# A two-layer graph network: where the node update's own half, its gate and its last elementwise steps are computed

## What is computed

```python
h = jnp.maximum(_layernorm(x, axis=-1), 0.0)
em = jnp.concatenate([h[src], h[dst]], axis=-1)
em = jax.nn.relu(layer_norm(em @ msg_w + msg_b, msg_g, msg_beta)) * edge_weights[:, None]
messages = segment_sum(em, dst) / (counts + 1e-08) * (counts > 0)
gate = jax.nn.sigmoid(h @ gate_w + gate_b)
combined = jnp.concatenate([h, messages], axis=-1)
h_new = jax.nn.relu(layer_norm(combined @ upd_w + upd_b, upd_g, upd_beta))
x = x + gate * h_new + (1.0 - gate) * h
```

## Time and profile before

| | us |
|---|---|
| median of 3 runs | 2472.26 (2470.81 to 2472.52) |
| the profiled execution, its own time | 2471.0 |
| its span in the trace | 2469.2 |
| attention layer's and message loop's gathers, busy on POOL | 1624.4 |
| busy: PE, DVE, ACT, POOL | 1646.5, 1522.7, 982.5, 1683.3 |
| mean granted TensorE clock | 0.85 of full |

### The profile page before, as it was taken

The page is one execution under the profiler, slowest core; times in us unless marked ns, Lnnn a source line. Parts: engine busy times, 40 slices in busy tenths (PEclk is TensorE's granted clock), DMA queues, the critical chain, the costliest instruction groups (busy, mean ns, idle before and its releaser), DMA issues.

```text
span 2469.2 us, 44266 instructions
## 1 busy us (share of the span) xinstructions
PE 1646.5 (67%) x9934; PEld 1201.4 (49%) x9934; DVE 1522.7 (62%) x4806; ACT 982.5 (40%) x3715; POOL 1683.3 (68%) x1718
## 2 busy tenths in 40 slices
PE   2387778777877777777456666666666666666650
PEld 2255555555555555555344454454454455544550
DVE  5455555555555555555647766666676666667668
ACT  3244334333434343434444444444444344434420
POOL 3377777777777777776017777777777777777732
PEclk9799889898988998999677888888788888889885
DMA  8544344444444344343244444433444444344321
GB/s 257 138 91 86 91 91 87 91 90 90 88 89 91 85 92 89 87 91 72 58 121 98 86 89 92 92 87 89 92 91 86 91 92 92 83 92 93 76 56 52
DMA packets 207823, 228.62 MB, mean 93 GB/s; under 512 B 103103, under 2 KB 153684, under 8 KB 207701
## 3 DMA queue, kind: packets, MB, share of 16 engines
q0 software_dynamic: 54784, 115.94, 24.0%
q1 hardware_dynamic: 152598, 110.34, 16.4%
q10 hardware_dynamic: 384, 1.70, 0.3%
HBM read 194.60 MB, written 33.24 MB: 92 GB/s over the span
## 4 chain that ended last, share of the span: by engine, by line
POOL 56%; issue 19%; PE 8%; DMA 7%; DVE 5%; SPq 1%; ACT 1%; POOLq 1%; ACTq 0%; DVEq 0%
POOL room L667 56%; DMA room<-src_table,rec 5%; PE psum L774 2%; PE psum L704 1%; PE psum L756 1%; PE psum L746 1%; DMA node_x<-in_x 1%; DVE room L1557 1%; PE psum L741 1%; DMA room<-state 1%; DVE stats L1127 1%; PE psum L835 1%; SPq L457 1%; PE psum L764 0%; ACT room L1000 0%
## 5 line engine op out<-in xcount | busy, mean ns | idle before, releaser
L667 POOL DMA_INDIRECT room<-src_table,rec x1664 | 1624.4, 976 | 684.1 <-issue 495.3
L835 PE MATMUL psum<-room,ident 128*128 128x384 f32 (+1 forms) x512 | 292.6, 659 | 377.4 <-DMA room<-src_table,rec 297.9
L1050 ACT ACTIVATE room<-psum 128x128 f32<-128x128 f32 x832 | 218.8, 274 | 585.6 <-DVE room L1478 583.2
L1316 DVE TENSOR_TENSOR room<-psum,room 128x384 f32<-128x384 f32 (+1 forms) x256 | 151.1, 590 | 455.6 <-ACT room L982 367.8
L982 ACT ACTIVATE room<-psum 128x384 f32<-128x384 f32 (+1 forms) x256 | 132.1, 516 | 560.5 <-PE psum L746 557.4
L1478 DVE TENSOR_TENSOR room<-psum,msg_g 128x384 f32<-128x384 f32 (+1 forms) x256 | 151.0, 590 | 315.0 <-PE psum L840 312.8
L746 PE MATMUL psum<-ident,room 128*128 128x128 f32 x832 | 155.4, 305 | 207.4 <-DMA room<-src_table,rec 206.9
L835 PEld LDWEIGHTS psum<-room,ident 128*128 128x128 f32 x512 | 93.1, 227 | 409.7 <-issue 384.7
L853 PE MATMUL psum<-room 128*125 128x128 f32 x1664 | 285.2, 318 | 1.5 <-ACT room L1062 1.5
L774 PE MATMUL psum<-room 128*125 128x128 f32 x1664 | 262.2, 300 | 18.9 <-ACT room L1000 6.3
L840 PEld LDWEIGHTS psum<-room 125*128 125x128 bf16 x2496 | 195.4, 112 | 140.8 <-issue 123.8
(11 more groups left out here) (179 smaller groups left out, 2122.6 us busy)
## 6 DMA issues: line engine op xcount, KB each, us to landing
room<-dst_perm SPq DMA_DIRECT2D x128, 406.2 KB
room<-src_table,rec POOLq DMA_INDIRECT x1664
room<-dst_table SPq DMA_DIRECT2D x128, 62.5 KB
src_table<-room SPq DMA_DIRECT2D x24, 224.0 KB
dst_table<-room SPq DMA_DIRECT2D x24, 224.0 KB
st_in<-state SPq DMA_DIRECT2D x64, 64.0 KB
state<-st_out SPq DMA_DIRECT2D x64, 64.0 KB
st_in<-state SPq DMA_DIRECT2D x64, 62.5 KB
```

What stands on the lines that cost most here:

```text
L667: pool.indirect_dma_start(out=xg[:, u, t * P:(t + 1) * P], out_offset=None, in_=src_table[n][:, :], in_offset=bass.IndirectOffsetOnAxis(ap ...
L835: nc.tensor.matmul(msg_bank[b][:, cols], ident[:, :], xg[:, u, t0 * P:t1 * P], start=True, stop=False, skip_group_check=True)
L1050: i = nc.scalar.activation(sq[:, j * P:(j + 1) * P], msg_bank[b][:, j * P:(j + 1) * P], ACT.Square, accum_out=var_e[:, c, j:j + 1])
```

## The change

The own half and the gate move in front of the message loop, behind the second tables. PE's `update_own` makes `h @ [upd_w own half | gate_w]`, 129 columns, into `rows_ps`; ACT's `gate_of` makes the gate from the last column; DVE's `own_part` makes `rest = 1 - gate`, overwrites `node_h` with `relu(node_h) * rest`, adds that to `node_x`, and then overwrites `node_h` with own half plus `upd_b`. PE's first message waits for all of it (`s_zh`), and ACT and DVE have it in front of their first pair. At the end `update` has only the message half, and `add_own` adds `node_h` in place of `upd_b`. The norm goes from DVE to ACT (`norm_out`), the product with the gate from POOL to ACT (`relu_out`: relu with the gate as scale, as the gate is positive) for groups 0 to 9, and to DVE for groups 10 to 12 (gate times the rows plus `node_x`, then the maximum with `node_x`). POOL has nothing left at the end. ACT makes the norm of groups 0 to 4 between its copies of groups 7 to 11, and the rest after the last square root. `upd_w` is loaded in two DMAs in place of one, and one memset of a column is gone.

The diff, cut to its core:

```diff
@@ sync @@
-            (upd_w[:, :, 0:D], a["L1_gnn_upd_w"].rearrange("(h k) f -> k h f", h=2)),
-            (upd_w[:, 0, D:D + 1], a["L1_gnn_gate_w"]),
+            (upd_w[:, 0:D], a["L1_gnn_upd_w"][0:D, :]), (upd_m[:, :], a["L1_gnn_upd_w"][D:2 * D, :]),
+            (upd_w[:, D:D + 1], a["L1_gnn_gate_w"]),
@@ gpsimd @@
-            pool.wait_ge(s_hrelu, 1)
-            for g, (t0, t1) in enumerate(GROUPS):
-                pool.tensor_tensor(node_x[:, t0:t1, :], node_x[:, t0:t1, :], node_h[:, t0:t1, :], ALU.add).then_inc(s_xh, 1)
-            for g, (t0, t1) in enumerate(GROUPS):
-                n = t1 - t0
-                pool.wait_ge(s_ur, g + 1)
-                ge(pool, s_fin, g - 1)
-                pool.tensor_tensor(ug[0:PP, g % 2, 0:n, :], ur[0:PP, g % 2, 0:n, :],
-                                   gate[:, t0:t1].unsqueeze(2).to_broadcast([PP, n, D]), ALU.mult).then_inc(s_uh, 1)
@@ tensor @@
-            pe.wait_ge(s_row, 2 * NG)
+            def update_own(g):
+                t0, t1 = GROUPS[g]
+                pe.wait_ge(s_row, 2 * NG)
+                ge(pe, s_zh, g - 1)
+                for t in range(t0, t1):
+                    i = nc.tensor.matmul(rows_ps[g % 2][0:PP, t - t0, 0:D + 1], feat_h[:, t, :], upd_w[:, :], start=True, stop=True)
+                i.then_inc(s_u, 1)
+            pe.wait_ge(s_wb, NWB * 16)
+            for g in range(NG):
+                update_own(g)
+            pe.wait_ge(s_zh, NG)
             all_pairs(pe, msg_slot, last, 1)
...
                 ge(pe, s_z, g - 1)
-                ge(pe, s_gate, g - 1)
                 for t in range(t0, t1):
-                    to = rows_ps[g % 2][0:PP, t - t0, 0:D + 1]
-                    nc.tensor.matmul(to, feat_h[:, t, :], upd_w[:, 0, :], start=True, stop=False)
-                    i = nc.tensor.matmul(to, mt[:, g % 2, t - t0, 0:PP], upd_w[:, 1, :], start=False, stop=True)
+                    i = nc.tensor.matmul(rows_ps[g % 2][0:PP, t - t0, 0:D], mt[:, g % 2, t - t0, 0:PP], upd_m[:, :],
+                                         start=True, stop=True)
@@ scalar @@
+            for g in range(NG):
+                gate_of(g)
             split_high(msg, 0, 0)
...
+            def norm_out(g):
+                t0, t1 = GROUPS[g]
+                act.wait_ge(s_norm_scale, 4 + (1 if t1 <= HALVES[0][1] else 2))
+                for t in range(t0, t1):
+                    i = nc.scalar.activation(msum[0:PP, t, :], msum[0:PP, t, :], ACT.Identity, bias=nmr[:, t:t + 1],
+                                             scale=rstd[:, t:t + 1])
+                i.then_inc(s_un, 1)
+            def relu_out(g):
+                t0, t1 = GROUPS[g]
+                act.wait_ge(s_ub, g + 1)
+                for t in range(t0, t1):
+                    i = nc.scalar.activation(msum[0:PP, t, :], msum[0:PP, t, :], ACT.Relu, scale=gate[:, t:t + 1])
+                i.then_inc(s_ur, 1)
+            FIRST = next(g for g in range(NG) if GROUPS[g][1] == HALVES[0][1]) + 1
             msg_features(0)
             for g in range(NG):
                 if g + 1 < NG:
                     msg_features(g + 1)
-                gate_of(g)
-                if t_end(g) == HALVES[0][1]:
+                if g == FIRST:
                     deviations(2, 0)
+                if g > FIRST and g - FIRST - 1 < FIRST:
+                    norm_out(g - FIRST - 1)
             deviations(2, 1)
+            for g in range(FIRST, NG):
+                norm_out(g)
+                if g - FIRST < RELU_ACT:
+                    relu_out(g - FIRST)
+            for g in range(NG - FIRST, RELU_ACT):
+                relu_out(g)
@@ vector @@
+            def own_part(g):
+                dve.wait_ge(s_gate, g + 1)
+                dve.tensor_scalar(rest[:, t0:t1], gate[:, t0:t1], -1.0, 1.0, ALU.mult, ALU.add).then_inc(s_rest, 1)
+                dve.wait_ge(s_rest, g + 1)
+                dve.scalar_tensor_tensor(out=node_h[:, t0:t1, :], in0=node_h[:, t0:t1, :], scalar=0.0,
+                                         in1=rest[:, t0:t1].unsqueeze(2).to_broadcast([PP, nt, D]), op0=ALU.max,
+                                         op1=ALU.mult).then_inc(s_held, 1)
+                dve.wait_ge(s_held, 2 * g + 1)
+                dve.tensor_tensor(node_x[:, t0:t1, :], node_x[:, t0:t1, :], node_h[:, t0:t1, :], ALU.add).then_inc(s_held, 1)
+                dve.wait_ge(s_held, 2 * g + 2)
+                dve.tensor_tensor(node_h[:, t0:t1, :], rows_ps[g % 2][0:PP, 0:nt, 0:D],
+                                  upd_b[0:PP, :].unsqueeze(1).to_broadcast([PP, nt, D]), ALU.add).then_inc(s_zh, 1)
...
-            dve.tensor_scalar(node_h[:, :, :], node_h[:, :, :], 0.0, None, ALU.max).then_inc(s_hrelu, 1)
...
             def finish(g):
-                dve.wait_ge(s_norm_scale, 4 + (1 if t1 <= HALVES[0][1] else 2))
-                for t in range(t0, t1):
-                    i = dve.tensor_scalar(un[0:PP, c, t - t0, :], msum[0:PP, t, :], rstd[:, t:t + 1], nmr[:, t:t + 1], ALU.mult, ALU.add)
-                i.then_inc(s_un, 1)
                 dve.wait_ge(s_un, g + 1)
+                dve.tensor_tensor(rows_g, rows_g, upd_g[0:PP, :].unsqueeze(1).to_broadcast([PP, nt, D]), ALU.mult).then_inc(s_ug, 1)
                 dve.wait_ge(s_ug, g + 1)
+                dve.tensor_tensor(rows_g, rows_g, upd_beta[0:PP, :].unsqueeze(1).to_broadcast([PP, nt, D]), ALU.add).then_inc(s_ub, 1)
-                dve.wait_ge(s_ub, g + 1)
-                ge(dve, s_uh, g - 1)
-                dve.scalar_tensor_tensor(out=ur[0:PP, c, 0:nt, :], in0=ub[0:PP, c, 0:nt, :], scalar=0.0, in1=node_h[:, t0:t1, :],
-                                         op0=ALU.max, op1=ALU.subtract).then_inc(s_ur, 1)
             def add_rows(g):
+                if g < RELU_ACT:
+                    dve.wait_ge(s_ur, g + 1)
+                    dve.tensor_tensor(node_x[:, t0:t1, :], node_x[:, t0:t1, :], rows_g, ALU.add).then_inc(s_fin, 1)
+                else:
+                    dve.wait_ge(s_ub, g + 1)
+                    for t in range(t0, t1):
+                        i = dve.scalar_tensor_tensor(out=msum[0:PP, t, :], in0=msum[0:PP, t, :], scalar=gate[:, t:t + 1],
+                                                     in1=node_x[:, t, :], op0=ALU.mult, op1=ALU.add)
+                    i.then_inc(s_held, 1)
+                    dve.wait_ge(s_held, 2 * NG + g - RELU_ACT + 1)
+                    dve.tensor_tensor(node_x[:, t0:t1, :], node_x[:, t0:t1, :], rows_g, ALU.max).then_inc(s_fin, 1)
             for g in range(NG):
                 finish(g)
-                if g > 0:
-                    add_rows(g - 1)
-            add_rows(NG - 1)
+                if g > 1:
+                    add_rows(g - 2)
+            for g in range(NG - 2, NG):
+                add_rows(g)
```

More of the change, by code:

```diff
@@ L107, in gnn_layers @@
         msg_beta = sb("msg_beta", [P, D])
-        upd_w = sb("upd_w", [P, 2, D + 1])
+        upd_w = sb("upd_w", [P, D + 1])
+        upd_m = sb("upd_m", [P, D])
         upd_b = sb("upd_b", [P, D])
@@ L120, in gnn_layers @@
         gate = sb("gate", [PP, NT])
+        rest = sb("rest", [PP, NT])
         factor = sb("factor", [PP, NT])
@@ L202, in gnn_layers @@
         mt = take(2 * GT * P).rearrange("p (u i f) -> p u i f", u=2, i=GT)
-        un = take(2 * GT * D).rearrange("p (u i f) -> p u i f", u=2, i=GT)
-        ug = take(2 * GT * D).rearrange("p (u i f) -> p u i f", u=2, i=GT)
-        ub = take(2 * GT * D).rearrange("p (u i f) -> p u i f", u=2, i=GT)
-        ur = take(2 * GT * D).rearrange("p (u i f) -> p u i f", u=2, i=GT)
         feat_y = feat_h
@@ L334, in gnn_layers @@
         s_ur = sem("s_ur")
-        s_uh = sem("s_uh")
-        s_xh = sem("s_xh")
+        s_rest = sem("s_rest")
+        s_held = sem("s_held")
+        s_zh = sem("s_zh")
         s_fin = sem("s_fin")
@@ L1072, in msg_slot, with gate_of @@
                         split_mid(msg, k + 1, (u + 1) % U)
+            def gate_of(g):
+                t0, t1 = GROUPS[g]
+                act.wait_ge(s_u, g + 1)
+                nc.scalar.activation(gate[:, t0:t1], rows_ps[g % 2][0:PP, 0:t1 - t0, D], ACT.Sigmoid,
+                                     bias=gate_b[0:PP, :]).then_inc(s_gate, 1)
+            for g in range(NG):
+                gate_of(g)
             split_high(msg, 0, 0)
@@ L1080, in msg_features @@
                 act.wait_ge(s_mtr, g + 1)
-                ge(act, s_u, g - 1)
+                ge(act, s_u, NG + g - 1 if g > 1 else 0)
                 nc.scalar.activation(mt[:, g % 2, 0:t1 - t0, 0:PP], turn_ps[g % 2][:, 0:t1 - t0, 0:PP], ACT.Copy).then_inc(s_mt, 1)
-            def gate_of(g):
+            def norm_out(g):
                 t0, t1 = GROUPS[g]
-                act.wait_ge(s_z, g + 1)
-                nc.scalar.activation(gate[:, t0:t1], rows_ps[g % 2][0:PP, 0:t1 - t0, D], ACT.Sigmoid,
-                                     bias=gate_b[0:PP, :]).then_inc(s_gate, 1)
```

(21 more changed lines are left out.)

14 lines of the change are left out of this document (4 added, 10 removed).

## The result

Median 2435.3 us (2433.72 to 2435.93, 4 runs) against 2471.53 (2469.22 to 2472.52) for the kernel before in the same comparison: ratio 0.9854, 95% interval 0.9837 to 0.9871, so 1.5% faster. The profiled execution took 2435.93 us, its span is 2434.1 us: 35.1 us less than before.

A forecast was written before the change was run, and what follows sets the result against it. POOL's gathers were taken to bound both loops, and state loads, PE and DVE the end. Span: 2469.2 - 0.6 - 5.4 - 25.4 + 1 = 2438.8 us; median 2441.9 us, 8-in-10 range 2436 to 2452.

The forecast's parts named there:

- The store behind it keeps its 8.4 us: After DVE's last addition: the stretch to the span's end is the last store and stays 8.4 us.
- POOL bounds nothing there: At the end of the kernel before: state loads, PE and DVE set the pace, not POOL; no size given.
- (c): Last scale to DVE's end (norm, gamma, beta, relu, final add): 57.26 us falls to 31.8, saving 25.4 us.
- the savings named for its low end: Low end of the forecast's own range, 2436 us: no cost at the gathers, the clock and the last stage's waits, 3.2 us.
- Own half in front of the loop: Before the message loop: DVE works 30 us, pair 0 comes 12 us late; a 37 us reserve makes the cost 0.
- The gathers beside it: Start of the message loop: 21 gathers run beside the own half, priced like the loop's at 0.5 us, taken as 1 us.
- The forecast's own sign of being wrong: Prediction is wrong if gathers beside the own half take well above 0.97 us.
- The rival's price: Gathers beside the own half: each of 21 held 0.69 us by a VectorE instruction, 15 us, giving 2456 us; chance 6%.
- (a): State loads to first update: the last scaling takes 1.48 us, not 2.13; updates start 0.6 us sooner.
- (b): First update to last scale: PE has half the passes, DVE sets 1.50 us a group; saves 5.4 us.
- The half clock: Update stage: PE may return at half clock after idling, 0 to 3 us, 0.5 taken; throughout, a rival at 2451 us, 5%.
- a rival with another price: Updates and last stage: ACT, with 90 norms and relus, becomes the bound; +5 us, 2447 us; chance 13%.

The follow-up runs named there:

- experiment 3: Changed kernel with checked count bounds plus one tiny GpSimd memset behind VectorE's last add: 3287.7 us, ratio 0.9934; 8.97 us behind the last add in place of 2.52.
- experiment 4: Kernel before with checked count bounds, its last two groups' product with the gate moved from GpSimd to VectorE: 3311.2 us, ratio 0.9993.
- experiments 5 and 8: Both on the second chip with checked count bounds: the changed kernel as control, 2436.6 us; the changed kernel with all 13 groups' relu on ScalarE, 2431.0 us.
- experiment 6: Changed kernel with checked count bounds and own half, gate and kept part moved behind the message loop: 2453.1 us, ratio 0.9927 to the kernel before.
- experiment 1: Controls on the first chip, loop counts read with checked bounds: the kernel before 3317.2 us (ratio 1.0015), the changed kernel 3287.7 us (ratio 0.9913).

## Why the prediction was right and where it wasn't

- **The step that failed: "The store behind it keeps its 8.4 us".** The 8.4 us behind DVE's last addition were put down to the last store, with no row for it, and the same forecast said of the end that "POOL bounds nothing there". In the kernel before the last store is over 2.3 us after DVE's last addition; what fills the rest is GpSimd's closing drain, which ends 8.6 us after GpSimd's last product, with the span's end 0.2 us behind it. Adding a memset of 0.10 us at the end of the changed kernel brings the long end back (8.97 us, experiment 3), and taking the last two products off GpSimd in the kernel before removes it (2.55 us, experiment 4). The change takes GpSimd's last work from 2460 to 2346 us, so the drain is over before DVE begins (c). With 2.6 in place of 8.4 us the sum would have been 2433.0 us of span, against 2434.1. The forecast priced what GpSimd's absence does to VectorE, and missed what it does to the end of the program.
- **From the span to the median: off by 1.9 us.** The forecast put the median 1.3 us above the profiled execution, as before; it came out 0.6 us below. Of the 6.6 us between forecast and median, 5.8 are the end and 1.9 are this; the other stages came out 1.1 us longer than forecast, the 2.4 us of a later start less what was gained elsewhere. With the end priced right the forecast would have been 2436.1 us against 2435.3, and part of that closeness is luck. The range was also set loosely: the savings named for its low end sum to 3.2 us, which gives 2438.7 and not 2436.
- **Own half in front of the loop: right.** 11 us late where 12 were forecast, and caught up; POOL's wait for TensorE in the loop is 7.6 us where it was 3.4, but that isn't the own half's doing: it is 5.5 and 2.4 us in experiments 5 and 8, which have the same own half, and 7.3 us in experiment 6, which has none in front. What it would cost without this cover is measured: 21.3 us (experiment 6).
- **The gathers beside it: right in the sum, mis-sized on the spot.** 1 us was taken from the loop's rows; the first 26 gathers took 2.65 us more. The forecast's own sign of being wrong, gathers "well above 0.97 us", did show: the 19 beside the own half take 1.09 us on average. The loop's row misled, as its instructions are mostly of kinds that didn't hold a gather in the own half: VectorE's `tensor_tensor` L1522 is busy 150.9 of the loop's 1057 us, 14%, while L1486 and L1488 are busy 1.38 of 2.40 us of a group. That this is the reason is likely, but no run tried it by itself. By the end of the loop 0.8 us were left, which is within what the runs scatter. The rival's price, a hold of 0.69 us for each of 21 gathers (15 us), is refuted; its mechanism isn't, as ten of 19 gathers were held for what was left of a VectorE instruction, 2.8 us in all. The Trainium skill (SBUF — State Buffer, Who interferes with whom) infers that VectorE's `tensor_tensor` leaves the descriptor work of a gather alone. The trace has gathers of 1.03 to 1.43 us that end 0.09 us after such an instruction, against 0.94 us, so here the measurement decides: it does hold them, and the `scalar_tensor_tensor` beside it doesn't.
- **(a): right.** 1.49 us for the scaling where 1.48 was forecast. The other 0.6 us of that stage's 1.2 came with the loads: the last scaling starts 29.5 us after the last gather, where it was 30.1. Why, no run shows.
- **(b): right.** 24.2 us where 23.8 was forecast. The half clock is there, as weighed, for two groups, and costs DVE 0.36 us where 0.5 was taken; the wait behind ScalarE's copies is 0.41 us where 0.3 was. As (b) varies by up to 1.6 us between runs of the same code (experiment 1), a hit within 0.4 us is in part luck.
- **(c): right in sum, from two errors.** 31.0 us where 31.8 was forecast. A relu takes 385 ns, where 382 was forecast and 388 was the estimate from the 93 ns for each pointer operand of the Trainium skill (ScalarE: Activation LUTs, What ACT_TABLE_LOAD costs); the trace agrees with the latter within 3 ns. ScalarE's work is 23.3 us (23 forecast), its round 2.71 us (2.7). VectorE's work fills 27.8 us (27.2 of them busy), where 30.1 was the sum, as a round of gamma, beta and addition takes 1.95 us and not 2.15; and its waits are 3.2 us, not 1.7. The first error made the forecast 2.3 us too long, the second 1.5 us too short. So ScalarE sets the first two thirds of the stage, which the forecast had as a rival with another price; the variant with 13 relus takes 3 us more off the stage, by ridding VectorE of its last products.

## What to carry to other kernels

Read what ends the span as a stage of its own: the last busy instruction isn't the end, and the chain may stop short of it. Look at the closing records of every engine's queue; the one that ends last says what a change there can win. Here an engine that was rid of its last small work near the end gave back more than its busy time, and one that got such a work paid for it. Work put in front of a loop under a reserve was nearly free here, but price it by rows of the same kind of instruction, not by the loop's mean. And when two instructions of different engines overlap, compare their end times before you call one slower: an end that follows another's by the same 0.09 us each time is a hold.

## What the runs showed of the hardware that was not expected

- GpSimd's closing drain ends 8.6 us after GpSimd's last instruction, whatever that is: a product of 0.99 us, a memset of 0.10 us or a gather. Where that comes last, the span ends 8.8 us after this instruction. Where it doesn't, the span ends 2.5 to 2.6 us after VectorE's last addition, and 3.4 to 3.5 us where several additions end back to back before it.
- A gather issued by GpSimd takes 0.94 us beside a quiet VectorE. Beside the own half's `tensor_tensor` instructions of 512 columns, with both inputs in SBUF or one in PSUM, it takes up to 1.44 us and then ends 0.08 to 0.10 us after one of them (135 of 136 long gathers). The `scalar_tensor_tensor` of the same size, with both inputs in SBUF, held none of 67.
- On two of three chips both kernels take 1.3 times as long, with the same 0.944 us for a gather; GpSimd waits for transfers that an ordinary chip has in time. (c), where VectorE and ScalarE work alone, is the same to 0.1 us on all three.
